# A convolution and mixture-of-experts kernel: other places for sixteen folds, a held back group of loads, and stores on a queue of their own

## The reference

```python
x = x + _L0_conv_ref(_ln_c(x), ...)          # layer norm, depthwise 3x3, pointwise, prunings
t = _to_tokens(x)                            # (16, 784, 128)
# _L0_ffn_ref(_ln_t(t), ...):
probs = jax.nn.softmax(x_flat @ Wr, axis=0)  # 8 experts
vals, idx = jax.lax.top_k(probs.T, 1024)     # each expert takes its 1024 best tokens
h = jax.nn.gelu(einsum('ecd,edf->ecf', x_flat[idx], W1) + b1, approximate=False)
out_e = einsum('ecf,efd->ecd', h, W2) + b2
output = zeros.at[idx].add(vals[..., None] * out_e)
t = t + output                               # and back to images
```

## Time and profile before

| | us |
|---|---|
| median of 3 runs | 471.27 (470.76 to 477.99) |
| the profiled execution, its own time | 471.32 |
| its span | 469.5 |
| busy: TensorE / VectorE / ScalarE / GpSimd | 359.3 / 329.2 / 257.1 / 157.2 |

### The profile page before, as it was taken

The page is one execution under the profiler, slowest core; times in us unless marked ns, Lnnn a source line. Parts: engine busy times, 40 slices in busy tenths (PEclk is TensorE's granted clock), DMA queues, the critical chain, the costliest instruction groups (busy, mean ns, idle before and its releaser), DMA issues. The chain is left out here.

```text
span 469.5 us, 8092 instructions
## 1 busy us (share of the span) xinstructions
PE 359.3 (77%) x2577; PEld 249.3 (53%) x2577; DVE 329.2 (70%) x1086; ACT 257.1 (55%) x528; POOL 157.2 (33%) x152
## 2 busy tenths in 40 slices
PE   2778998999999879301148799996998989778752
PEld 2435655666556657200113568766484847637642
DVE  3478788898999886788887697776486342335744
ACT  3469898899998873566701665752343433520000
POOL 4000000000000000010037777787778887766100
PEclk9989999999999995555555999998799989979955
DMA  4456577767676644899902232357986449969897
GB/s 110 128 143 194 159 237 255 227 225 229 201 240 235 194 147 140 261 390 328 320 23 54 54 100 78 76 80 165 296 240 124 86 41 267 290 111 216 260 370 292
DMA packets 42323, 89.07 MB, mean 190 GB/s; under 512 B 7568, under 2 KB 18992, under 8 KB 42288
## 3 DMA queue, kind: packets, MB, share of 16 engines
q1 hardware_dynamic: 32224, 76.62, 51.3%
q0 software_dynamic: 8576, 8.72, 11.0%
q10 hardware_dynamic: 1488, 3.30, 1.8%
HBM read 41.45 MB, written 36.81 MB: 167 GB/s over the span
## 5 line engine op out<-in xcount | busy, mean ns | idle before, releaser
L776 PE MATMUL psC<-x_pad,tap_diag 64*64 64x392 f32 x384 | 68.2, 501 | 8.9 <-issue 5.1
L776 PE MATMUL psC<-hid,tap_turned 64*64 64x392 f32 x384 | 68.2, 501 | 0.0
L503 POOL TENSOR_TENSOR logits_T<-top,logits_T 112x896 f32<-112x896 f32 x1 | 1.7, 1682 | 197.7 <-ACT top L660 197.7
L948 PE MATMUL psC<-w,hid 128*128 128x128 f32 x448 | 52.8, 277 | 1.8 <-ACT hid L702 1.7
L948 PEld LDWEIGHTS psC<-w,hid 128*128 128x128 f32 x448 | 51.0, 192 | 3.9 <-ACT hid L702 3.0
L702 ACT ACTIVATE hid<-psB,b_T 128x512 f32<-128x512 f32 x32 | 21.9, 687 | 53.9 <-PE psB L936 53.9
L776 PEld LDWEIGHTS psC<-x_pad,tap_diag 64*64 64x64 f32 x384 | 28.0, 135 | 37.6 <-issue 28.7
L472 POOL DMA_INDIRECT picked<-token_rows,slot_idx x32 | 31.3, 979 | 45.7 <-issue 44.8
L936 PE MATMUL psB<-picked_T,w 128*128 128x512 f32 x64 | 37.6, 719 | 6.5 <-DVE x_all L1452 3.3
L580 ACT ACTIVATE ln_tok<-psA,sm 112x128 f32<-112x128 f32 x112 | 40.9, 477 | 0.9 <-DVE sm L1089 0.9
L1437 DVE TENSOR_TENSOR y_sum<-psC,b_rows 128x512 f32<-128x512 f32 x14 | 9.6, 688 | 39.3 <-PE psC L948 39.3
(11 more groups left out here) (280 smaller groups left out, 873.3 us busy)
## 6 DMA issues: line engine op xcount, KB each, us to landing
token_rows<-rows SPq DMA_DIRECT2D x16, 422.6 KB, 4.9
x_in<-in_x_dram SPq DMA_DIRECT2D x16, 392.0 KB, 3.4
x_res<-in_x_dram SPq DMA_DIRECT2D x16, 392.0 KB, 4.0
moe_sum<-hid SPq DMA_DIRECT2D x16, 392.0 KB, 4.5
x_all<-work SPq DMA_DIRECT2D x16, 392.0 KB, 3.0
moe_sum_mid<-hid SPq DMA_DIRECT2D x16, 392.0 KB, 5.7
moe_sum_late<-hid SPq DMA_DIRECT2D x16, 392.0 KB, 4.8
w<-in_L_ffn_W_dram SPq DMA_DIRECT2D x16, 256.0 KB, 3.1
```

Source lines behind the costliest of these rows:

```text
L776: ins = nc.tensor.matmul(psC[col * HC:col * HC + HC, half, 0:HALF].rearrange("c (h w) -> c h w", w=W), weights[of, n, :], lines[of, q, dy: ...
L948: ins = nc.tensor.matmul((psA if first else psC)[:, h, b * C:(b + 1) * C], hid[:, f, lo:lo + 128], w2[:, q, f * C:(f + 1) * C], start=(f = ...
```

## The change

Three edits.

1. The mid folds are split in three: image 0 directly behind expert 7's first hidden layer (TensorE) and ahead of its bias (VectorE); images 1 and 2 behind the first outputs; images 3 to 15 behind the second outputs. VectorE now normalizes the second half's rows ahead of folds 1 and 2, where it did so behind six folds.
2. SP issues the mid loads of images 0 to 2 as before, and those of 3 to 15 only when gather(7,1) has landed.
3. SP stores nothing: ScalarE's queue stores all sixteen images, the first of them after the eighth block of expert 7 has landed.

```diff
-MID_FOLDS = 6
-STORED_BY_SP = 8
+FOLDS_AT_LAST = (range(0, 1), range(1, 3), range(3, B))
+STORES_AMONG_BLOCKS = 1
...
             for img in range(B):
+                if img == FOLDS_AT_LAST[1].stop:
+                    sp.wait_ge(s_gat[1][(E - 1) % BUFS], (E - 1) // BUFS * (8 * SB) + 8 * SB)
                 sp.wait_ge(s_fd, 2 * img + 2)
                 load_sums(mid_t, img)
...
             for img in range(B):
                 load_late(img)
-                if img >= B - STORED_BY_SP:
-                    stored = img - (B - STORED_BY_SP)
-                    sp.wait_ge(s_fa, stored + 1)
-                    sp.dma_start(out_d[:, ds(stored, 1), :], o_img[stored % ENDS]).then_inc(s_fo[stored % ENDS], 16)
...
+            def store_image(img):
+                act.wait_ge(s_fa, img + 1)
+                act.dma_start(out_d[:, ds(img, 1), :], o_img[img % ENDS]).then_inc(s_fo[img % ENDS], 16)
+
             for b in range(SB):
                 act.wait_ge(s_blk[b], 16)
                 act.sem_inc(s_landed, 1)
-            for img in range(STORED_BY_SP, B):
-                act.wait_ge(s_fa, img + 1)
-                act.dma_start(out_d[:, ds(img, 1), :], o_img[img % ENDS]).then_inc(s_fo[img % ENDS], 16)
+                if b >= SB - STORES_AMONG_BLOCKS:
+                    store_image(b - (SB - STORES_AMONG_BLOCKS))
+            for img in range(STORES_AMONG_BLOCKS, B):
+                store_image(img)
...
                 hidden(e, q, 0, {})
+                for img in FOLDS_AT_LAST[0]:
+                    turn_sums(1, img)
                 pe.wait_ge(s_w2[q], use * 16 + 16)
                 down(e, q, 0)
-                for img in range(MID_FOLDS):
+                for img in FOLDS_AT_LAST[1]:
                     turn_sums(1, img)
                 turn_picked(e, 1)
-                pe.wait_ge(s_fk, 2 * (B + MID_FOLDS))
+                pe.wait_ge(s_fk, 2 * (B + FOLDS_AT_LAST[1].stop))
                 hidden(e, q, 1, {})
                 down(e, q, 1)
-                for img in range(MID_FOLDS, B):
+                for img in FOLDS_AT_LAST[2]:
                     turn_sums(1, img)
...
+                    if h == 0:
+                        for img in FOLDS_AT_LAST[0]:
+                            add_sums(1, img)
                     bias_out(e, h)
                     weigh(e, q, use, h)
-                    for img in (range(MID_FOLDS), range(MID_FOLDS, B))[h]:
-                        add_sums(1, img)
                     if h == 0:
                         norm_picked(e, 1)
+                    for img in FOLDS_AT_LAST[1 + h]:
+                        add_sums(1, img)
```

## The result

Executions of both kernels spread over some ten microseconds (before 468.1 to 478.0, after 471.2 to 478.9, 22 of each). The ratio of the changed kernel to the one before is 1.0097, 95% interval 1.0071 to 1.0123: 1% slower, where 0.4% faster was forecast. This ratio counts only executions within 1.5% of the fastest of their kernel, which leaves out eight of the 22 before and two of the 22 after; over all of them the medians are 473.8 and 474.4 us (0.1% apart) and the means 473.3 and 474.8 us (0.3%). So it is sure that the forecast gain is missing, and the size of the loss, between 0.1 and 1%, hangs on how the executions are counted. The profiled execution has a span of 471.2 us (before 469.5). The result is within 2%, as the chances said, but with the wrong sign.

A forecast was written before the change was run, and what follows sets the result against it. From 388 us, GpSimd's issue train and the DMA bytes bound it side by side. Last block at 440.2, plus 25.5 of bytes, 1.8 of tail and 1.8 between span and time: 469.3 us; range 463.5 to 474.5.

The forecast's parts named there:

- Part 1, the folds: Expert 7's second half: fold 0 costs nothing, normalization starts at 408.1 not 413.77, second half 5.6 us earlier, rows ready about 423.
- Part 2, the quiet gather: With mid loads held, gather(7,1) lands at 402.9, not 407.6; GpSimd's 1.38 us wait for expert 5's blocks shrinks by 1.1.
- The landing that starts scatter(7): Expert 6's last block, issued at 414.7, lands 6.3 us later at 421.0, against 419.87 before; bounds 418.8 to 422.0.
- the last landing itself: Expert 7's last block lands 6.1 us after its issue at 434.1, so at 440.2 against 441.4 before.
- the issue train: GpSimd's scatter(7) from first to last issue: 7 x 1.86 = 13.0 us, against 15.4 before, without the 2.65 us wait.
- Part 3, the bytes: After the last block, 8 late loads and 16 stores, 9.6 MB at 377 GB/s, take 25.5 us, plus 1.8 of tail.
- The end itself: From the last block's landing at 440.2 to the end at 467.5: 25.5 us of bytes plus 1.8; 28.1 before.
- the ramp: The slower stretch after the last block's landing, 231 GB/s up to 444 before; claimed to go in the changed kernel.
- One of the prediction's own signs of being wrong: After the last block: a stretch after 441 under 300 GB/s would show it wrong, over 340 from 442 right.
- the byte debt decides: Rival at the late loads' start: first goes at 427 not 423.2, 3.8 us never come back; time 473 to 475; chance 0.16.
- the row wait goes whole: Rival at expert 7: 5.67 us of folds come off or expert 6's landing stays 4.1 us; time 466.5; chance 0.22.
- The stores' own queue gives nothing: Rival at the end: last block at 440.2, then 28.1 us as before; time 470.1; chance 0.17.

The follow-up runs named there:

- the single part: Only the stores changed against the kernel before: SP's eight stores taken out, all sixteen in ScalarE's queue; ratio 0.9982 (0.9940 to 1.0023).
- The best version: The changed kernel without the wait of mid loads, with four stores among the counting of expert 7's blocks in place of one; ratio 0.9921 to the kernel before.

## Why the prediction was wrong

*Part 1, the folds: right.* No cost for fold 0, the normalization directly behind the weighting, no wait for weighted rows. The normalization began at 411.74, not at 408.1, because TensorE was later in this execution: expert 6's last rows were weighted at 401.4, before at 397.6. From there it came after 10.4 us (before 16.1), 5.7 us sooner where 5.6 was forecast. The clock, which I let be cold, stayed at full in 403 to 423 (granted 1.00; before 0.63 from 415 to 423), and the four hidden matmuls took 1.98 us and not 3.75; nothing came of it, since GpSimd was later still. A slip without effect: by its own figures the prediction had GpSimd ask for the rows at 421.0 + 4 x 1.86 = 428.4, 5.4 us behind them, not four; it was 7.4.

*Part 2, the quiet gather: right.* Forecast 2.6 us from issue to landing, measured 2.5 to 3.0; scatter(6) went out 0.3 us behind the gather.

*The landing that starts scatter(7): the step that failed.* "Landing by the low bound 4.1 gives 418.8, by the high 7.3 gives 422.0; I take 6.3": from issue to the next scatter it was 8.7 in the changed kernel, 8.8, 9.1 and 9.3 in the others with the thirteen loads held ahead of this block, above my upper bound. Two things were wrong in the term. The 4.1 was not a landing: it runs from issue to the next issue, and the chain of the kernel without the wait has 3.31 us of landing in its 4.10:

```profile
416.59 3.31 DMA moe_sum_late<-y_rows,slot_idx
420.69 1.55 POOL moe_sum_late L488
```

The other 0.8 us pass between the landing and GpSimd's next scatter; 6.3 and 7.3, which are landings, lack them. And the landing itself took 7.93 us beside the held loads, 1.6 more than I took and 0.6 more than the gather that gave the bound. Why an accumulating block takes longer than a gather there is not shown; it landed as the loads ran out: the engines' rate was 271 GB/s in 422 to 424 and 26 in 424 to 426.

These 2.4 us are nearly the whole miss of the profiled execution. From expert 5's first scatter (385.91 before), the forecast has the last issue of scatter(6) at 28.8 us, the last block's landing at 54.3 and the end at 81.6; measured were 28.8, 57.4 and 84.1. Of the 3.1 us at the last landing, 2.4 are this term and 0.7 the last landing itself (6.8 us, not 6.1); the issue train took the 13.0 us that were forecast, and the end was 0.6 us shorter.

*Part 3, the bytes: the terms right, the balance not drawn.* I had the debt as 5.6 loads, 2.25 MB (measured 4.25 - 1.95 = 2.3 MB), and set against it the idle window of 415 to 423. But filling that window opened the next: with expert 6's block late, no late load could start before 428.06 (forecast 426), and 423 to 432 ran at 134 GB/s. A hole can't be filled by moving work into it when the work behind it waits for the same landing. The end itself was near its term: 26.7 us from the last block, forecast 27.3, although the way there was another: the ramp was full as forecast, but full of loads alone. One of the prediction's own signs of being wrong came: over 340 GB/s were forecast from 442 on, and 294 to 307 were moved until 450.

*The rival "the byte debt decides"* named this mechanism and its place, and had the late loads 3.8 us later; from expert 5's first scatter they were 3.7 us later (41.0 against 37.3). It had 0.16. That its time, 473 to 475, holds the median of 474.4 is in part luck: it was counted from 471.3, and the kernel before had a median of 473.8 in the same set. The second half of its condition, an end longer than 27 us, did not come (26.7). I gave it little since a window was seen to be idle, and did not ask what the bytes behind that window would wait for. Of "the row wait goes whole" nothing was seen; it needed the 4.1 us to stay, which they did only in the kernels that hold seven mid loads or none (4.0 to 4.2). "The stores' own queue gives nothing" comes out as the single part does: 0.9982.

*What stays open.* The profiled executions show 0.5 us between the two kernels from expert 5's first scatter on, less than two executions of one kernel differ by, and the ratio 1%, some 4.6 us; over all executions the medians are 0.6 us apart and the means 1.5. With and without the wait (folds and stores as changed) the profiled stretches are 84.1 against 80.7 and 79.9, 3.4 to 4.2 us, where the ratios show 1.3 to 1.5%, 6 to 7 us; the medians of all executions show 0.6 to 0.7%, some 3 us, about what the profiles do. The cost of the wait in this kernel is thus better put at 3 to 4 us than at 7. For the change against the kernel before, no profile shows a loss of the ratio's size. Why the stores are a loss with the wait and a small gain without was not settled.

## What to carry to other kernels

Holding transfers back to let a short one through is paid for in the bytes that don't move meanwhile, unless a later idle window is truly free: ask what the transfers behind that window wait for. Hold as few as keep the engines busy until the held moment: with thirteen loads held the stretch to the end was some 3 us longer than with seven. And a gain on a chain of waits is worth no more than the wait of the engine that it feeds: 2.65 us here, of 5.67. Take a term of a sum from rows that measure the same thing: from issue to landing and from issue to the next issue differed by 0.8 us here.

## What the runs showed that I had not expected

Stores in a queue of their own did not share the engines evenly with loads queued before them. In the changed kernel the first store took 8.0 us with seven late loads still on the way, and 300 GB/s, the rate of loads alone, was moved until 450; with the loads held back the same store took 2.4 us. The rate depends on what is moved: about 300 GB/s for these loads alone, 408 to 418 with stores in the mix (450 to 458), 403 to 406 for stores alone (462 to 468). It would follow that stores started early earn more than loads started early. The best version starts its stores early, but the step to it from the kernel without the wait (0.9970 to 0.9921) lies inside the intervals, so this is not shown.
